# Moving the first copy of k and the mask work of layer 0 from ScalarE to VectorE

## The reference

```
q = Wq @ x + bq;  k = Wk @ kv + bk;  v = Wv @ kv + bv
attn = softmax(where(kv_mask, (q * 0.25)^T k, -inf))
mean = attn v;  ex2 = attn (v * v);  std = sqrt(relu(ex2 - mean * mean))
xn = (x*m - mean_x) / sqrt(relu(var_x) + 1e-5)      # per channel over positions, m the mask
out = (xn * std + mean) * m
```

## Time and profile before

| | us |
|---|---|
| median of 3 runs | 1853.46 |
| lowest and highest | 1851.41, 1853.76 |
| the profiled execution's own time | 1851.41 |
| its span, first to last instruction | 1849.6 |
| PE busy in the span | 1727.6 (93%) |
| VectorE busy | 1336.3 (72%) |
| ScalarE busy | 1111.6 (60%) |
| GpSimd busy | 353.3 (19%) |

### The profile page before, as it was taken

How to read it: one execution, slowest core, us unless ns; L and a number is a source line. 1 busy time by engine, 2 the same in 40 slices (tenths; PEclk the granted TensorE clock), 3 DMA queues, 4 the chain that set the end, 5 groups by cost and what they waited for, 6 DMA issues and landing times. The chain is left out here.

```text
span 1849.6 us, 34340 instructions
## 1 busy us (share of the span) xinstructions
PE 1727.6 (93%) x12328; PEld 1194.2 (65%) x12328; DVE 1336.3 (72%) x2795; ACT 1111.6 (60%) x2469; POOL 353.3 (19%) x427
## 2 busy tenths in 40 slices
PE   6999999999999997899989988999999599999998
PEld 2344433344343343788778777888887499999997
DVE  3778888888888745899898988899999653333322
ACT  1667676776768656777767877777777451111111
POOL 0002130211213131322232222232222040000000
PEclk7899999999999988999999999999999799999999
DMA  3011011110100122222233523333332140000000
GB/s 107 11 36 50 16 47 29 38 48 16 48 17 25 57 79 75 75 71 70 70 77 90 137 66 97 87 92 96 90 100 73 52 137 13 11 11 11 15 15 17
DMA packets 75688, 105.03 MB, mean 57 GB/s; under 512 B 21392, under 2 KB 36240, under 8 KB 75280
## 3 DMA queue, kind: packets, MB, share of 16 engines
q1 hardware_dynamic: 65040, 82.08, 16.1%
q0 software_dynamic: 8192, 16.79, 3.7%
q10 hardware_dynamic: 2304, 4.20, 0.8%
HBM read 39.55 MB, written 4.72 MB: 24 GB/s over the span
## 5 line engine op out<-in xcount | busy, mean ns | idle before, releaser
L466 DVE TENSOR_REDUCE nmax<-ps 128x2 f32<-128x1024 f32 x256 | 311.2, 1220 | 117.0 <-PE ps L357 116.0
L642 ACT ACTIVATE prob<-ps 128x1024 f32<-128x1024 f32 x256 | 261.8, 1022 | 163.8 <-PE ps L369 162.8
L1422 ACT ACTIVATE at_prob<-at_t,at_nmax 128x256 f32<-128x256 f32 x512 | 256.5, 505 | 108.4 <-DVE at_nmax L1225 99.4
L384 PE MATMUL ps<-prob,v 128*64 128x512 f32 x1024 | 279.0, 623 | 0.0
L1225 DVE CUSTOM_DVE_ANT_0 at_t<-at_t,at_off 128x256 f32<-128x256 f32 x512 | 236.7, 499 | 8.8
L1744 ACT ACTIVATE mlp_h<-ps,b 128x256 f32<-128x256 f32 x128 | 53.8, 472 | 270.2 <-PE ps L1679 270.2
L1783 DVE CAST mlp_h_hi<-mlp_h 128x512 fp32r<-128x512 f32 x64 | 29.4, 459 | 221.1 <-ACT mlp_h L1744 221.1
L1580 POOL TENSOR_TENSOR at_low<-at_low,at_high 128x512 fp32r<-128x512 f32 x64 | 85.6, 1338 | 499.1 <-DVE at_high L1251 499.1
L1056 PE MATMUL ps<-ident,at_prob 128*128 128x128 f32 x1024 | 159.3, 279 | 1.4 <-ACT at_prob L1422 1.4
L1045 PE MATMUL ps<-at_k_stack,at_q_stack 96*128 96x256 f32 x512 | 118.9, 315 | 37.8 <-ACT at_prob L1422 32.2
L1679 PE MATMUL ps<-mlp_x_hi,mlp_w_hi 128*128 128x256 f32 x512 | 145.8, 285 | 6.5 <-DVE mlp_w_lo L1768 6.5
(11 more groups left out here) (203 smaller groups left out, 4323.0 us busy)
## 6 DMA issues: line engine op xcount, KB each, us to landing
at_k_stack<-at_high SPq DMA_DIRECT2D x256, 64.0 KB, 2.4
at_q_stack<-at_high SPq DMA_DIRECT2D x128, 64.0 KB, 2.7
at_q_stack<-at_high POOLq DMA_DIRECT2D x128, 64.0 KB, 2.4
at_q_stack<-at_low SPq DMA_DIRECT2D x128, 64.0 KB, 2.2
at_k_stack<-at_low POOLq DMA_DIRECT2D x128, 64.0 KB, 2.3
mlp_w_in<-in_w SPq DMA_DIRECT2D x32, 256.0 KB, 3.1
c_in<-in_ctx SPq DMA_DIRECT2D x8, 512.0 KB, 4.6
X<-in_x SPq DMA_DIRECT2D x8, 512.0 KB, 5.2
```

Of the source, the lines that this page charges most:

```text
L384: mm = eng.matmul(ps[2 * QD * k:2 * QD * (k + 1), VB, :], v[:, c, HG * G + 2 * p + k, :], prob[:, M % PROBS, k, :], start=(c == 0), stop=( ...
L466: eng.tensor_reduce(nmax[:, n % 2, j, 2 * p:2 * p + 2], ps[:, at:at + 2, :], AX, ALU.max, negate=True).then_inc(s_max, 1)
L642: eng.activation(prob[:, M % PROBS, :, :], ps[:, ST:ST + 2, :], ACT.Exp).then_inc(s_exp, 1)
L1422: ins = eng.activation(prob[:, m % 2, i, :], t[:, p, i, :], ACT.Exp, scale=-1.0, bias=nmax[:, m % 4, i:i + 1], accum_out=z[:, T % 2, j, 2 ...
```

## The change

`masks` and `high_k` move from ScalarE's program to VectorE's. k1 is now a tensor_scalar from PSUM, right before `raw_k` in slot 5; the mask cast and `far` are a tensor_copy and a tensor_scalar in slot 1 of group 3 of the batch before (for the first batch, at the start). VectorE no longer waits for ScalarE's `far`, and waits for itself instead where it reads what it has just written. The semaphores `s_far` and `s_masked` go; the last mask counts on VectorE's own chain.

```diff
-        def rest_k(n):
+        def masks(b):
+
+            eng.tensor_copy(mask[b % 3][:], m_in[:, b, :]).then_inc(s_mask, 1)
+            eng.wait_ge(s_mask, b + 1)
+            if b:
+                eng.wait_ge(s_k2, NG * b)
+            eng.tensor_scalar(far[:], mask[b % 3][:], row[:, FAR_AT:FAR_AT + 1], row[:, FAR_OFF:FAR_OFF + 1],
+                              ALU.mult, ALU.add).then_inc(links.sem, 1)
+            eng.wait_ge(links.sem, links.after())
+
+        def high_k(n):
+            made(eng, "k", n)
+            if n >= RING:
+                eng.wait_ge(s_st, 8 * (n - RING) + 8)
+            eng.tensor_scalar(k1[:, n % RING, :], ps[:, MB, :], b0[:, 1, n % NG:n % NG + 1], None, ALU.add)\
+               .then_inc(s_k1, 1)
             eng.wait_ge(s_k1, n + 1)
             eng.scalar_tensor_tensor(out=raw_k[:], ...
         def low_k(n):
             taken(eng, "k", n)
-            if n % NG == 0:
-                eng.wait_ge(s_far, n // NG + 1)
...
         # the loop of VectorE
                     if s == 5:
-                        rest_k(w + 1)
+                        high_k(w + 1)
...
                 if w % NG == 3 and b < NB:
+                    if s == 1 and b + 1 < NB:
+                        masks(b + 1)
...
         # ScalarE: both functions and their calls go
-        eng.wait_ge(s_bits, DMA)
-        masks(0)
-        high_k(0)
...
-                if s == 5 and w + 1 < GROUPS:
-                    high_k(w + 1)
-                if s == 7 and w % NG == 2 and b + 1 < NB:
-                    masks(b + 1)
```

More of the change, by code:

```diff
@@ L195, in layer0 @@
         s_mask = sem("mask")
-        s_far = sem("far")
-        s_masked = sem("masked")
         s_stat = sem("stat")
@@ L537, in last_mask @@
             eng.wait_ge(s_fin, FINISH * (b + 1))
-            eng.tensor_tensor(X[:, b, h, :], X[:, b, h, :], mask[b % 3][:], ALU.mult).then_inc(s_masked, 1)
-            eng.wait_ge(s_masked, SB * b + h + 1)
+            eng.tensor_tensor(X[:, b, h, :], X[:, b, h, :], mask[b % 3][:], ALU.mult).then_inc(links.sem, 1)
+            eng.wait_ge(links.sem, links.after())
             eng.bn_stats(six[:], X[:, b, h, :]).then_inc(links.sem, 1)
@@ L549, in vector @@
         eng.tensor_copy(ident_r[:], ident[:])
-        rest_k(0)
+        eng.wait_ge(s_bits, DMA)
+        masks(0)
+        high_k(0)
         low_k(0)
@@ L642, in exponentials @@
             eng.activation(prob[:, M % PROBS, :, :], ps[:, ST:ST + 2, :], ACT.Exp).then_inc(s_exp, 1)
[L644 to L662, removed]
         def take_q(n):
```

## The result

| | us |
|---|---|
| before, median of 5 runs beside it | 1853.46 (1850.83 to 1853.76) |
| after, median of 5 runs | 1867.82 (1862.28 to 1869.4) |
| ratio, 95% interval | 1.008 (1.0062 to 1.0097) |
| the profiled execution of after | 1857.01, span 1855.2 |

A forecast was written before the change was run, and what follows sets the result against it. PE was taken to set the pace, chained almost back to back. Terms summed to +6.3 us on the profiled 1851.41, giving 1857.7; with the median 2.05 above, 1859.8, range 1855 to 1867.

The forecast's parts named there:

- start: Before the first q copy: ScalarE's table load becomes exposed, +1.28, raw_k starts earlier, -0.3; net +1.0 us.
- group 0: First head group of layer 0: PE waits for raw_k, so the whole new k1 copy is paid, +0.7 us.
- kind 0: Groups 8, 12, ... 28 of layer 0: next scores wait for a later k2, 0.6 in each of six, +3.6 us.
- kind 1: Groups 9 to 29, every fourth: raw_k ends later, so v products start 0.2 late, six times, +1.2 us.
- group 2: Layer 0's group numbered 2 from 0: the one gain counted among groups with number mod 4 of 2, -0.2 us.
- kind 2: Groups with number mod 4 of 2: earlier exponentials offset by waits for maxima; 0 for six, ends -1.2 and +2.1 us.
- kind 3: Groups with number mod 4 of 3, also given the masks: v 0.3 late, absorbed in PE's 0.82 wait; 0 us.
- Rival B: Third and fourth groups of batches: mask work meets GpSimd, stretches and makes VectorE the bound; 1868 us, chance 0.17.
- Rival A: PE's waits for exponentials: relief of ScalarE shrinks them and wins; 1852.1 us, chance 0.06.
- Rival C: k1 copy on VectorE costs only the low end, 0.42: +3.1, 1856.6 us, no change that can be told; chance 0.20.

The follow-up runs named there:

- preload: The changed kernel plus one tiny ScalarE activation ahead of the first q copy, so the table load comes early; 1859.75, 1861.04 and 1861.96 us in three runs.
- k0_back: Against preload, k1 back on ScalarE for the groups whose k is made in groups of kind 0; 1856.3 us, ratio 1.0015 to before.
- k2_back: Against preload, k1 back on ScalarE only where it is made in groups of kind 2; 1858.7 us, ratio 1.0036 to before.
- before_again: The kernel before, unchanged, run again as a control and for a second profile; 1852.92 us, ratio 0.9995.
- before_preload: The kernel before with one small ScalarE activation ahead of its wait for the mask DMA; 1852.08 us, ratio 1.0001.
- masks_only: Against before, only the mask work moves to VectorE, k1 stays on ScalarE, table load exposed; 1853.14 us, ratio 1.0005.
- k1_only: Against before, only k1 moves to VectorE, mask work and hidden table load stay on ScalarE; 1858.64 us, ratio 1.0036.

## Why the prediction was wrong

Term by term, in us:

| step | forecast | measured | by |
|---|---|---|---|
| start | 1.0 | 1.2 by the waits; 3.1 by the place of the first turn; 1.6, 2.4 and 4.9 in the medians | timeline; 6 profiles against 12; preload against after, three times |
| group 0 | 0.7 | 0.8 | v's wait, 1.13 to 1.92 |
| kind 0 | 3.6 | 4.0 | periods; k0_back |
| kind 1 | 1.2 | 1.3 | periods |
| group 2 | -0.2 | -0.25 | period, 19.28 to 19.03 |
| kind 2 | 0 | 2.4 pooled, 2.3 in the medians; nothing in the changed kernel's own four profiles | 9 profiles against 9; k2_back |
| kind 3, with group 3 | 0 | 1.3 | periods |
| sum | 6.3 | 11.1 to 14.4 | the four comparisons of after with before |

With 1.2 for the start the measured terms add up to 10.8, with 3.1 to 12.7. The steps that were worked from a chain of waits held: the exposed load, group 0, kinds 0 and 1, group 2. Those on VectorE came out a tenth above the forecast, because k1 took 0.75 and not 0.68, the price of raw_k beside it; of the ends given, the upper one was right. The 0.04 for the wait on its own semaphore came out as put (366.43 + 0.74 to 367.21). The mask work came out near its price, the cast at 0.43 for 0.63 and far at 0.55 for 0.42.

Three terms were too low: kind 3 and kind 2, both put at 0, and the start. Only the loss in kind 3 shows in every profile of the changed kernel.

In kind 2 the step that failed is "I take 0 for the sum of six". The mechanism was named there: x_lo 0.2 later, past GpSimd's start in a third batch, 0.7. I read the three late batches of one profile as a property of the batches and the flip as one event. They are draws: GpSimd's start scatters by over 1 us, x_lo has moved 0.25 into it, and the chance of being late went from 14 in 54 to 27 in 54. And the price of a late group was taken from before, a wait of 0.64. It was 1.47 with one more k1 in the chain, and a clock fall followed in 3 of 27. The profiles show how little one of them says here: in after's own four, 2, 1, 1 and 4 groups were late, in preload's three 5, 4 and 5. That gap between two kernels that differ only at the start is larger than chance would often give, and nothing here explains it. It also limits the term. In after's own four profiles the six periods add up to 115.3 us on average, in those of before, before_again and before_preload to 115.7, in preload's three to 118.5. So the 2.4 is a mean over all kernels with k1 on VectorE in kind 2; that the changed kernel's timed executions paid it is likely, but not shown.

Kind 3 failed in the sentence that v's delay vanishes in the wait of 0.82. v's did, though it was 0.95 and not 0.3; but I had followed only k1 and the masks, not what they push against GpSimd, nor the relu of the deviation, which ends the chain that PE then waits for. Rival B had the right mechanism on the wrong instruction: it looked whether the masks meet GpSimd's first products (they don't) and not whether q1's last step, two calls later, meets the second ones. The halves agree: in masks_only that step is stretched to 1.85 (group 19) and the period stays 21.31; in k1_only it takes 0.74 and the period stays 21.31 (five of six; the sixth holds a fall of the clock); with both it is 21.48. VectorE had room for either and not for both. That the stretch itself is needed for the loss is an estimate, as no kernel has both halves without it: it adds 0.75 to q1's step, in masks_preload the relu came 0.54 earlier in the one group without it (27), and here it came 0.17 too late.

The Trainium skill's "GPSIMD Engine Reference", section "Specifications", says that GpSimd's SBUF interfaces are shared with VectorE and contend with its instructions of two SBUF inputs. The stretched x_lo and q1 agree. What decided this case is the order of the two starts, of which that section says nothing. x_lo beside GpSimd's product was stretched only where it began behind it, in 108 of 108 groups.

Rival A was wrong as argued: the waits for exponentials did shrink, 9.4 to 2.5, and hardly any time came of it (0.25 us in group 2, 0.12 in each early group of kind 2). Rival C fell with the price of k1.

**Open.** The start's part beyond what its waits show, the third term that was too low. In the six profiles with an exposed load the turn of group 0 stood at 52.5 us on average, in the twelve with a hidden one at 49.4, which is 1.8 more than the load. Half of that is in PE's q product, 3.4 to 3.8 us long in five of the six and in three of the twelve, 2.0 to 2.6 else. But in five of the six that product ends before the load begins (in masks_only the load stands ahead of it), so the load can't have caused it in that execution. The granted clock doesn't tell either: over the product it reads 1.00 in after, where it took 3.78, and in before_again, where it took 1.98. It may be chance.

**A better version.** masks_preload, the mask work on VectorE with the load hidden and every k1 left on ScalarE, beat the kernel before in both of its comparisons, by 2.7 and 4.8 us (ratios 0.9983, 0.997 to 0.9995, and 0.9974, 0.9964 to 0.9984), and the changed one, beside it, by 15.9. The second gain is more than the 2 to 3 us expected, and where either comes from is not shown.

## What to carry to other kernels

Where a wait ends with two engines meeting by chance, one profile is one draw: look at how far the two starts lie apart in every batch, and price a shift by how many draws it turns, at the cost of the chain as it will be, not as it was. When work is moved onto an engine, follow each instruction that it pushes back and ask what that one now meets, and check the two halves of a change for room that each uses up alone. And when the first instruction of an engine is taken away, its hidden table load moves to the next one; a tiny activation ahead of the first wait hides it again (the load at 0.75 us instead of 20.29).

## What the runs showed of the hardware

The stretch is nearly all or nothing, and its border is sharp to some hundredths: 0.03 us after GpSimd's start x_lo took 0.68, 0.05 after it 1.78. The border isn't one and the same for all instructions: q1's last step took 1.85 where the profile has it 0.03 ahead of GpSimd's start (masks_only), and 0.74 where it has it 0.05 ahead (masks_preload, group 27), and GpSimd's own spans are rough. A tensor_scalar from PSUM to fp32r with a pointer as its scalar took 0.74 to 0.75 on VectorE, as much as raw_k with its second input, and not the 0.683 of a plain copy. And the granted clock fell to its lower level after single waits of 1.46 to 1.48 us in a stream that was otherwise dense, but 24 others like them had no fall behind them, so the wait alone does not decide it.
